# Grouped attention: q's rotation and split moved to pair 8, k's rotation and split folded over 128 partitions, GpSimd's row passes moved to pairs 2 and 3

## The reference

```python
h = _rmsnorm(hidden_states, ln1_w)
q = (h @ Wq).reshape(b, s, H, HD)      # H = 16 heads of HD = 8
k = (h @ Wk).reshape(b, s, HKV, HD)    # HKV = 4
v = (h @ Wv).reshape(b, s, HKV, HD)
q = _apply_rope(q, cos, sin)
k = _apply_rope(k, cos, sin)
...
attn = jax.nn.softmax(scores, axis=-1)          # causal
attn_out = ctx @ Wo
h = jnp.clip(residual + attn_out, -100.0, 100.0)
...
topv, topi = jax.lax.top_k(probs, K)            # 2 of 8 experts a token
```

## Time and profile before

| what | value |
|---|---|
| median of 3 runs (lowest to highest) | 3167.33 us (3165.84 to 3172.26) |
| the profiled execution, its span | 3168.82 us, 3167.1 us |
| PE, DVE, ACT, POOL busy in the span | 91%, 78%, 73%, 67% |
| grouped attention | about 503 to 1283 us of the span |

### The profile page before, as it was taken

How to read it: one execution, slowest core, us unless ns; L and a number is a source line. 1 busy time by engine, 2 the same in 40 slices (tenths; PEclk the granted TensorE clock), 3 DMA queues, 4 the chain that set the end, 5 groups by cost and what they waited for, 6 DMA issues and landing times. The chain is left out here.

```text
span 3167.1 us, 66396 instructions
## 1 busy us (share of the span) xinstructions
PE 2893.0 (91%) x22314; PEld 1882.3 (59%) x22314; DVE 2458.5 (78%) x6944; ACT 2318.5 (73%) x3601; POOL 2118.8 (67%) x2432
## 2 busy tenths in 40 slices
PE   6999996898888988789579999999999999999979
PEld 3666653444444444678246666666666666666658
DVE  5667666787887874667568888888888888888867
ACT  5888872566655657444279999999999999999933
POOL 6777763346555543677658787878787887788744
PEclk8999997899999989899789999999999999999989
DMA  4554444221222230585400000000000000000001
GB/s 122 131 131 114 114 116 85 58 65 45 69 68 57 56 69 19 181 277 159 131 1 1 17 1 17 1 7 11 5 13 1 17 1 17 1 17 1 1 14 41
DMA packets 151510, 178.32 MB, mean 56 GB/s; under 512 B 18619, under 2 KB 122784, under 8 KB 151076
## 3 DMA queue, kind: packets, MB, share of 16 engines
q1 hardware_dynamic: 142084, 157.14, 19.0%
q0 software_dynamic: 9088, 16.94, 1.5%
HBM read 99.82 MB, written 75.95 MB: 55 GB/s over the span
## 5 line engine op out<-in xcount | busy, mean ns | idle before, releaser
L3397 PE MATMUL lb_FF<-lb_h,lb_w 128*128 128x512 f32 x1024 | 501.2, 592 | 0.0
L3626 DVE TENSOR_SCALAR lb_z<-lb_M,lb_mv,lb_rstd 128x128 f32<-128x128 f32 x1024 | 344.8, 398 | 3.3 <-POOL lb_rstd L3551 3.0
L3514 ACT ACTIVATE lb_h<-lb_H,lb_prm 128x512 f32<-128x512 f32 x512 | 326.6, 697 | 2.6 <-PE lb_H L3388 2.6
L3551 POOL TENSOR_TENSOR lb_rstd<-lb_rstd,half 128x4 f32<-128x4 f32 x256 | 260.4, 1017 | 36.9 <-issue 0.9
L3382 PE MATMUL lb_H<-lb_x1s,lb_w 128*128 128x512 f32 x512 | 272.2, 532 | 0.8 <-issue 0.8
L3397 PEld LDWEIGHTS lb_FF<-lb_h,lb_w 128*128 128x128 f32 x1024 | 193.5, 189 | 89.5 <-issue 60.8
L544 ACT ACTIVATE ga_PT<-ga_S 128x384 f32<-128x384 f32 x256 | 111.6, 488 | 179.0 <-PE ga_S L355 178.9
L3618 DVE BATCH_NORM_STATS2 lb_stats<-lb_M 128x6 f32<-128x128 f32 x1024 | 227.0, 284 | 13.0 <-PE lb_M L3341 7.9
L3388 PE MATMUL lb_H<-lb_x1s,lb_w 128*128 128x512 f32 x512 | 202.9, 397 | 0.1
L3383 PE MATMUL lb_H<-lb_x1s,lb_w 128*128 128x512 f32 x512 | 202.8, 396 | 0.0
L3569 POOL CAST lb_x1s<-lb_x 128x512 fp32r<-128x512 f32 x128 | 78.0, 609 | 175.1 <-DVE lb_x L3651 175.1
(11 more groups left out here) (516 smaller groups left out, 8896.7 us busy)
## 6 DMA issues: line engine op xcount, KB each, us to landing
moe_w<-experts_dram SPq DMA_DIRECT2D x39, 384.0 KB, 3.4
da_qT<-da_stq SPq DMA_DIRECT2D x64, 192.0 KB
da_kT<-da_stk SPq DMA_DIRECT2D x64, 192.0 KB, 3.7
moe_x<-moe_xs SPq DMA_DIRECT2D x39, 260.0 KB, 3.6
tc_g<-moe_ys SPq DMA_DIRECT2D x32, 256.0 KB, 3.8
ga_q<-ga_stq SPq DMA_DIRECT2D x20, 384.0 KB, 5.8
lb_split<-moe_parts SPq DMA_DIRECT2D x8, 896.0 KB
da_stq<-da_parts SPq DMA_DIRECT2D x16, 384.0 KB, 2.4
```

The source lines that it names most:

```text
L3397: pe.matmul(FF[:, :], w2[:, k, :], h[:, k, :], start=(k == 0), stop=(k == KC - 1)).then_inc(ff_filled, 1)
L3514: act.activation(h[:, k, :], H[:, k % 2, :], ACT.Gelu_apprx_tanh, bias=col(FB1 + k, i)).then_inc(h_ready, 1)
L3551: pool.tensor_tensor(out[:, :], out[:, :], C["half"][:, 0:NT], ALU.pow).then_inc(done, 1)
L3626: last = v.tensor_scalar(z[:, t, :], M[:, t * P:(t + 1) * P], mv[:, t, 0:1], rstd[:, t:t + 1], ALU.subtract, ALU.mult)
```

## The change

k is folded: columns 0 to 255 of its projection go to partitions 0 to 63 of `M`, columns 256 to 511 to partitions 64 to 127, and the sum of halves puts each 128-token block on its own 32 partitions. So `rotate_k` is 128x256, and `copy_sum`, `split_k` and `third_k` are 128x128. `store_k` becomes twelve DMAs, three a block, and two tables in the folded shape are loaded at the stage's start. `rotate`, `split_q` and `third_q` run one body earlier, for `b+3` in pairs 7 and 8, POOL's two steps ahead of the scatters of these pairs. POOL's `scales`, `normalise` and `residual` move from pairs 4 and 6 to pairs 2 and 3, and DVE's `measure` that feeds them to pair 6 of the body before. `choose` is cut in two, with its last three operations as `mark` in pair 3.

```diff
         wout = sb("wout", [P, P])
-        wq, wk, wv, rope, k_rope, pair_sum = (
-            G[n] for n in ("wq", "wk", "wv", "rope", "k_rope", "pair_sum"))
+        wq, wk, wv, rope = (G[n] for n in ("wq", "wk", "wv", "rope"))
+        k_rope = sb("k_rope", [P, SEQ // 2])
+        pair_sum = sb("pair_sum", [P, KV * HD])
...
         rotB = sb("rotB", [P, SEQ])
-        rotK = sb("rotK", [2 * KV * HD, SEQ])
-        restK = sb("restK", [KV * HD, SEQ])
+        rotK = sb("rotK", [P, SEQ // 2])
+        restK = sb("restK", [P, P])
         partsQ = sb("partsQ", [P, 3, SEQ], BF16)
-        partsK = sb("partsK", [KV * HD, 3, SEQ], BF16)
+        partsK = sb("partsK", [P, 3, P], BF16)
...
             def project_kk(c):
                 bank_free()
-                pe.matmul(M[0:2 * KV * HD, :], wk[:, :], xnT[:, :], start=True, stop=True
-                          ).then_inc(kk_filled, 1)
+                for half in range(2):
+                    last = pe.matmul(M[64 * half:64 * half + 64, 0:SEQ // 2], wk[:, :],
+                                     xnT[:, SEQ // 2 * half:SEQ // 2 * (half + 1)],
+                                     start=True, stop=True)
+                last.then_inc(kk_filled, 1)
...
             def sum_k(c):
                 bank_free()
-                pe.matmul(M[0:KV * HD, :], pair_sum[:, :], rotK[:, :], start=True, stop=True
-                          ).then_inc(k_summed, 1)
+                pe.wait_ge(fold_loaded, 32)
+                for t in range(NT):
+                    r = slice(64 * (t // 2), 64 * (t // 2) + 64)
+                    last = pe.matmul(M[32 * t:32 * t + 32, 0:P], pair_sum[r, :],
+                                     rotK[r, t % 2 * P:(t % 2 + 1) * P], start=True, stop=True)
+                last.then_inc(k_summed, 1)
...
             def copy_sum(c):
...
                     act.wait_ge(k_split, c - 1)
-                act.activation(restK[:, :], M[0:KV * HD, :], ACT.Copy).then_inc(sum_copied, 1)
+                act.activation(restK[:, :], M[:, 0:P], ACT.Copy).then_inc(sum_copied, 1)
...
             residual(1)
+            rotate(1)
+            third_q(1)
...
-                    if s == 0 and exists(c2):
-                        rotate(c2)
                     if s == 1 and exists(c2):
-                        third_q(c2)
                         third_k(c2)
-                    if s == 3 and 2 <= c3 < NB:
+                    if s == 1 and exists(c3):
...
                         normalise(c3)
-                    if s == 5 and 1 <= c3 < NB:
+                    if s == 2 and exists(c3):
...
                         make_rows(p)
+                    if s == 6 and exists(c3):
+                        rotate(c3)
+                    if s == 7 and exists(c3):
+                        third_q(c3)
...
             def rotate_k(c):
                 v.wait_ge(kk_filled, c)
-                v.tensor_tensor(rotK[:, :], M[0:2 * KV * HD, :], k_rope[:, :], ALU.mult
+                v.wait_ge(fold_loaded, 32)
+                v.tensor_tensor(rotK[:, :], M[:, 0:SEQ // 2], k_rope[:, :], ALU.mult
...
                 if c > 1:
-                    v.wait_ge(k_stored, 48 * (c - 1))
+                    v.wait_ge(k_stored, K_STORES * (c - 1))
...
                                 ).then_inc(gap_ready, 1)
+
+            def mark(r):
+
...
             v.tensor_copy(matsb[:, :, :], mats[:, :, :])
+            split_q(1)
+            measure(2)
             for b in range(-1, NB + 1):
-                p, c, c2, c3, r = b - 1, b + 1, b + 2, b + 3, b - 2
+                p, c, c2, c3, c4, r = b - 1, b + 1, b + 2, b + 3, b + 4, b - 2
...
                         take_max(m, 1)
-                    if s == 0 and exists(c2):
-                        split_q(c2)
...
                         choose(r)
-                    if s == 2 and 2 <= c3 < NB:
-                        measure(c3)
+                    if s == 2 and exists(r):
+                        mark(r)
+                    if s == 5 and exists(c4):
+                        measure(c4)
+                    if s == 7 and exists(c3):
+                        split_q(c3)
...
                     sp.wait_ge(k_loaded, 32 * (c - 2))
-                sp.dma_start(stk[c % 2, :, 0:3, :], partsK[:, 0:3, :]).then_inc(k_stored, 16)
-                sp.dma_start(stk[c % 2, :, 3:5, :], partsK[:, 0:2, :]).then_inc(k_stored, 16)
-                sp.dma_start(stk[c % 2, :, 5:6, :], partsK[:, 0:1, :]).then_inc(k_stored, 16)
+                for t in range(NT):
+                    r, cols = slice(32 * t, 32 * t + 32), slice(t * P, (t + 1) * P)
+                    sp.dma_start(stk[c % 2, :, 0:3, cols], partsK[r, 0:3, :]).then_inc(k_stored, 16)
+                    sp.dma_start(stk[c % 2, :, 3:5, cols], partsK[r, 0:2, :]).then_inc(k_stored, 16)
+                    sp.dma_start(stk[c % 2, :, 5:6, cols], partsK[r, 0:1, :]).then_inc(k_stored, 16)
...
 
+            sp.dma_start(k_rope[:, :], C["k_rope_halves_dram"]).then_inc(fold_loaded, 16)
+            sp.dma_start(pair_sum[:, :], C["pair_sum_halves_dram"]).then_inc(fold_loaded, 16)
```

More of the change, by code:

```diff
@@ L60, in grouped_attention @@
     ROWS_AT = (0, 3, 1, 2)
+    K_STORES = 16 * 3 * NT
     LAST_MAX = 24 * NB - 1
@@ L120, in grouped_attention @@
         ones_loaded = sem("ones_loaded")
+        fold_loaded = sem("fold_loaded")
         scales_ready = sem("scales_ready")
@@ L1026, in load_k @@
             def load_k(c):
-                sp.wait_ge(k_stored, 48 * c)
+                sp.wait_ge(k_stored, K_STORES * c)
                 for e in range(2):
@@ L3875 @@
     }
+    arrays["k_rope_halves"] = np.concatenate([arrays["k_rope"][:, :T // 2], arrays["k_rope"][:, T // 2:]], 0)
+    arrays["pair_sum_halves"] = np.tile(arrays["pair_sum"], (2, 1))
     nc = bacc.Bacc("TRN2", target_bir_lowering=False, num_devices=1)
```

## The result

The changed kernel takes 3149.84 us (median of 6 runs, 3145.69 to 3160.26), the kernel before 3169.98 us on the same chip (6 runs); the ratio is 0.9941, 95% interval 0.9922 to 0.9961. It is faster by 0.6%, some 20 us, where the prediction's sum was 50.7: the sign is right, the size is not, and the time lies outside the range. The profiled execution took 3145.69 us, span 3144.0, 23.1 less than the profiled one of before.

What follows compares the result with a forecast made beforehand. It took DVE's wait for q's sum behind GpSimd's scatters, with its clock loss, as the bound. Bodies go from 46.47 to 42.5 us; 3168.8 less 50.7 and 1.5 gives 3117 us, range 3100 to 3142.

Steps and rivals of the forecast that it cites:

- What bounds the kernel: Pairs 1 to 3: DVE ends last, waiting for q's sum behind GpSimd's scatters; the stall also lowers the clock.
- Pairs 2 and 3, -1.85 us: Without q's split and with a small k split, these pairs go from 11.94 to 10.1 us a body.
- Pairs 8 and 1, +0.15: q's split, now in pair 8, delays later DVE work; 0.15 us a body reaches PE, between 0 and 0.6.
- Pair 4, +0.2 us: PE waits about 0.4 us for `mark` ahead of `rank`; cost 0.2 us a body, between 0 and 0.6.
- Pair 5, +0.3 us: Twelve stores of k make the loads land at about 804.3, PE needs k at 803.8; cost 0.3 us a body.
- slack of 3.9 us: Pair 5 before: DMA engines quiet at 804.0, PE needing k at 807.91; the forecast used this margin up.
- The whole: Gains of 39.7 us in bodies 3 to 12, 7.1, 4 and 2.4 in others, less 2.5: 50.7 us.
- +2.5 forecast: Body -1: nine more stores on the chain to the first k, less an earlier, shorter split, cost 2.5 us.
- (a): Rival: k's stores take 1 to 4 us longer, PE stands in pair 5 of some twelve bodies; 3129 to 3160 us; 20%.
- (b): Rival: scatters hold q's split, or GpSimd's passes hold `choose` and `mark`; 1.5 us a body, 3135 us; 8%.
- (d): Rival: no change, the wait only moves, DVE standing in pair 8 for q's sum; 4 us a body, 3167 us; 4%.

Runs made afterwards that it cites:

- q_only: The kernel before with only q's sum, split and third part moved one body ahead into pairs 7 and 8; 3109.06 us, ratio 0.9812.
- k_four: The changed kernel with k's six slots laid out on chip by two more VectorE copies, four stores instead of twelve; 3111.37 us, ratio 0.982.
- no_fold: The changed kernel without the fold of k: k handled as before, with three stores; 3112.42 us, ratio 0.9809.
- k_four_mark: The changed kernel with four stores of k and the marking back behind the choice in pair 2; 3100.39 us, ratio 0.9777.
- no_fold_mark: The changed kernel without the fold of k (three stores) and with the marking back in pair 2; 3106.27 us, ratio 0.980.
- k_eight_mark: k_four_mark with each of k's four stores cut in two, so eight stores of the same bytes; 3105.47 us in one execution.
- mark_back: The changed kernel with the marking back behind the choice in pair 2, all else as changed; 3154.82 us in one execution.
- after_again: The changed kernel run once more, unchanged; 3151.12 us, ratio 0.9944.
- after_pad: The changed kernel with 15 drains ahead of VectorE's loop over the bodies, no work added; 3146.03 us in one execution.
- k_four_passes: k_four_mark with the statistics and GpSimd's row passes back in their old pairs 3, 4 and 6; 3104.89 us.
- q_first: The changed kernel with q's loads issued ahead of k's twelve stores; 3142.26 us in one execution.

## Why the prediction was wrong

- **What bounds the kernel**: right. q's sum behind the scatters was the loss; q_only, which moves nothing else, takes it all, and the clock falls in one of its bodies 3 to 12 instead of in all ten.
- **Pairs 2 and 3, -1.85 us**: right, 4.68 and 5.43 us. **Pairs 8 and 1, +0.15**: nothing, 4.72 and 5.40 us against 4.74 and 5.40.
- **Pair 4, +0.2 us**: mis-sized, 0.75 us (4.89 to 5.64). PE waited 0.88 us for the marks in body 7, not 0.4. In bodies 4 and 11 the clock fell there (3.4 us from 749.97 and 1050.35), and pair 4 took 6.46 and 6.34 us. Back in pair 2 the marks leave that pair at 4.68 us, take 1.1 us off pair 4 and add 0.3 to pair 3 (k_four and no_fold against k_four_mark and no_fold_mark).
- **Pair 5, +0.3 us**: this step failed; it measured 1.2 us (5.69 to 6.89). Its times were near: last store issued 13.5 us into the body (13.6 to 14.7 in bodies 3 to 12), loads landing at 21.9 (22.2 in the mean), PE there at 21.4 (22.0). But it took the moment at which the DMA engines fall quiet for the one at which PE may go on. PE goes on at k's last signal, at 22.9 us in the mean, 0.7 after the last packet. So PE stood in all ten bodies, 1.02 us in the mean, which is most of the 1.2. The slack of 3.9 us that I read in before was 2.9: in its body 5 the last signal comes at 804.80, not at 804.0, and PE waits for it ahead of the mask at 807.68, not at the product of 807.91. On top of it the clock fell behind the longest waits, 1.92 and 1.82 us in bodies 7 and 12; I had read in before that a stall is paid twice, and reckoned this one once. k_four and no_fold, and k_eight_mark against mark_back, show that the twelve issues are the cause: with fewer the slack is there.
- **The whole**: bodies 3 to 12 gave 32.7 us instead of 39.7, bodies 1 and 2 gave 2.2 instead of 2.4, body 13 gave 4.4 instead of 7.1 (its pair 5 took 9.37 us). Body 0 gave 1.2 instead of 4 in this execution, where the clock stood low from 565.65 to 582.72; in after_again it took 40.34 us, 4.2 less than before. Body 0's start moved by 4.1 us, 1.3 of it ahead of the stage (+2.5 forecast).
- **Not in the sum**: the last stage, +8.9 us. I took the stages that the change doesn't touch as unchanged; the changed kernel has 15 more VectorE instructions than before, and after_pad shows that shifting the code by 15 takes the 8.9 us away again.
- **Rivals**: (a) names what happened: PE stood over 1 us for k in five of the bodies 1 to 13. Its condition did not come, as the last store was issued 0.5 us and the loads landed 0.3 us later than reckoned in the mean, and not 1 to 4. That its range (3129 to 3160) holds the result is partly luck, since pair 4 and the last stage are in it too. Of its two grounds the lost slack was the right one. The Trainium skill, DMA: Bandwidth & Descriptors, section Specifications, would charge k's 256-byte runs; the runs do not show it: k_four_mark, with the same runs as the changed kernel, has the loads landed as early as no_fold_mark with 1024-byte runs (18.5 to 19.5 and 18.4 to 19.9 us into bodies 3 to 12). (b) and (d) are refuted: q's casts took 0.43 us in bodies 3 to 12 and waited for nothing.

## What to carry to other kernels

Count what a rearranged tile costs in DMA issues: the fold made k's arithmetic shorter, but with the nine more issues of 0.47 us that it brought the stage loses 23 of the 59 us that it gains without the fold (720.4 and 743.6 against 779.5). Read the slack of a load from its last signal to the first instruction that waits for it, and not from the moment at which the DMA engines fall quiet. Where a sum uses that slack up, price the wait behind it with what the clock takes. When an untouched stage changes its time, look for one late instruction that the new code has moved there, and shift the code before explaining it otherwise.

## What the runs showed of the hardware

- A wait of TensorE of 1.9 us was followed, 1.3 us after its end, by 3.4 us at a granted clock of 0.50, and cost 3.4 us in all. Over all the profiles above, the clock fell at each of the 26 waits of 1.77 us and more ahead of pair 5's mask (bodies 1 to 13), at six of the ten of 1.05 to 1.67 us, and at none of up to 1.0 us; in three pairs 5 (q_only, bodies 2 and 8, and k_four_passes, body 2) it fell without such a wait.
- The last signal of a load came 0.5 to 1.0 us after its last packet, and TensorE went on 0.09 us after the signal (changed kernel, bodies 3 to 13).
- One gap of 0.28 us on VectorE, at a place that recurs every 128 instructions of its stream, changed a steady cycle for eight tiles (7.20 to 7.97 us each). The fourth normalising step takes 0.34 us alone and about 1.1 beside GpSimd's pass of 1.04; the Trainium skill, SBUF — State Buffer, section "SBUF: two separate sides", has GpSimd or VectorE (in some of its instructions) hold the shared ports for a whole instruction, and this trace agrees. Why VectorE starts late at these places no row shows.
- Small stores put on a queue behind a large load were written only 3.6 us after the last of them was issued (q_first).
